# Attention probabilities transposed in twenty 64-row pieces instead of ten whole blocks

## The chip, the cores and the metric

The kernel runs on one core of one Trainium2 chip. Times are device microseconds of the whole program. The core's engines are TensorE (PE for its matmuls, PEld for its weight loads), VectorE (DVE), ScalarE (ACT), GpSimd (POOL) and SyncE (SP); they run side by side and meet at semaphores.

## The reference, cut to what matters

A block of a graph network on 625 nodes of 512 features, in two layers with a mixture of experts between them. Three stages of it are attention over all nodes with 8 heads of 64: one of the first layer's expert block, and two of the graph transformer, in which the sum over edges is taken as a masked attention over all 625 x 625 pairs of nodes.

```
q = (x @ Wq + bq).reshape(b, s, H, HD)
k = (x @ Wk + bk).reshape(b, s, H, HD)
v = (x @ Wv + bv).reshape(b, s, H, HD)
scores = jnp.einsum('bqhd,bkhd->bhqk', q, k) / jnp.sqrt(jnp.float32(HD))
attn = jax.nn.softmax(scores, axis=-1)
o = jnp.einsum('bhqk,bkhd->bqhd', attn, v).reshape(b, s, d) @ Wo + bo
...
hp = h @ weight
msgs = hp[src] * edge_weight[:, None]
agg = jax.ops.segment_sum(msgs, dst, num_segments=h.shape[0])
```

All of it is in fp32. The second excerpt is a sum over 20000 edges; the kernel builds a matrix of counts and weights out of the edge list, on which both the sum and the masks of the later attention rest.

## The kernel before

The 625 nodes are cut into NC = 5 chunks of NP = 125 rows. A stage of attention (`attention`, defined once for each engine, called with a = 0 for the expert block and with a = 1 and 2 for the graph transformer) handles the heads in PAIRS = 4 pairs and the nodes in 5 chunks, so it has 20 rounds u. For each round there are two score tiles `Sx[u % 3][h]` of 125 x 625, one for each head h. TensorE's order in round u is written out by hand:

- `scores(u + 2)`: q times k of both heads into PSUM banks 0 to 2 (L828). The heads lie on rows 0 to 63 and 64 to 127 of the array.
- `projection(i + 1, n)`: one or two pieces of the next pair's q, k and v (L805, L810). In the last pair of a stage (rounds u = 15 to 19) there is none.
- in the last two rounds `early`, a product of the stage behind (L624 in the first stage, L1033 in the others).
- `context(u - 1)`: the transposed probabilities times v (L859), two heads in the two column halves of the array, into bank 5.
- `turned(u)`: the probabilities transposed, five blocks of 125 x 125 for each head. Four of each head go to bank 3 + h (L841), the fifth ones to bank 5 (L848). A transpose is a matmul whose weights are the block and whose moving operand is the identity.

VectorE runs in round u `scaled(u + 1)` (L1630 to L1635, probabilities times the reciprocal sum), `largest(u + 2)` (L1622, scores with the mask out of PSUM, and their extreme), the values of the next pair, and `context_out(u - 1)` (L1642). ScalarE runs `turned_out(u - 1)` (L1241 twice and L1245: the transposed blocks out of PSUM into `PT`), then `exponentials(u + 2)` (L1233) and parts of the projections. The semaphores that matter here: `prob` (a head's probabilities are ready), `pT` (transposes written), `pTc` (copied out), `av` and `ctx` (context written, copied out). The first transposes into bank 3 + h wait for the copies out of the same bank, those into bank 5 for the copy out of bank 5 and for `ctx`.

The edge windows are another part. At the start VectorE works out, for each of NW = 20 windows of target nodes, the first and the last tile of edges; `window_ranges` (L350 to L356) loads these 2 x 20 values into registers on TensorE's and on VectorE's queue. TensorE does so behind the product `hp` (L624), VectorE behind the operations that make the one-hot rows (L1505). Then comes the loop over windows: VectorE makes a one-hot tile (L1516) and TensorE multiplies it (L682, L692).

After an attention stage the gates of the experts are a product with `gateW` and `gateW1` (L907), 32 columns of weights each and a padding of zeros.

## Time and profile before

| | |
|---|---|
| time, median of 3 runs | 1142.01 us (1137.84 to 1142.13) |
| the profiled execution, span from first to last instruction | 1134.8 us |
| TensorE busy | 1087.0 us, 96% |
| weight loads busy | 728.6 us, 64% |
| VectorE busy | 560.2 us, 49% |
| ScalarE busy | 371.2 us, 33% |
| GpSimd busy | 126.9 us, 11% |
| granted TensorE clock, mean | 1.000 |

The page of the profile gives busy times and a chain of work that ended last. The timeline gives groups of like instructions in order of time: start, time from the first one's start to the last one's end, engine, line, operation and count; in brackets the idle time before the group and what ended it. Ends of matmuls are modelled, so groups that follow each other seem to overlap by some 0.2 us: the starts are what one reads. PEldq and DVEq are the queues (sequencers) of TensorE and VectorE, which fetch values, check and branch.

### The profile page before, as it was taken

The numbers are of one execution on the slowest core, as the hardware profiler recorded it, in microseconds if no ns is written. First come the engines' busy times: TensorE is split into PE (matmuls) and PEld (weight loads), VectorE is DVE, ScalarE is ACT, GpSimd is POOL, SyncE is SP. The second block draws the span as 40 slices with busy tenths as digits, with TensorE's granted clock in tenths as the row PEclk, the third lists the DMA queues.
The fourth block names the chain that finished last, engine by engine and source line by source line (L and its number), as shares of the span: only waits on it lengthen the run. The fifth ranks groups of instructions, "written<-read, shape, count | busy, mean of one in ns | idle before, by whom it ended". The sixth has DMA issues, their size and how long they took to land.

```text
span 1134.8 us, 20059 instructions
## 1 busy us (share of the span) xinstructions
PE 1087.0 (96%) x7339; PEld 728.6 (64%) x7340; DVE 560.2 (49%) x1409; ACT 371.2 (33%) x931; POOL 126.9 (11%) x183
## 2 busy tenths in 40 slices
PE   3899999999999988999999899999999999999999
PEld 2588646468777554455545577887577778755764
DVE  7999738645445421121211444553324455587641
ACT  1012212035555412122212445453124455412630
POOL 1045460020000020010101530000000000001000
PEclk9999999999999999999999999999999999999999
DMA  4100475000000379800899840000210100000001
GB/s 133 38 1 3 131 201 213 1 28 29 19 11 1 155 248 409 332 14 18 330 400 403 295 167 29 29 29 1 75 56 29 29 29 1 1 37 1 1 3 43
DMA packets 21402, 112.69 MB, mean 99 GB/s; under 512 B 5127, under 2 KB 6904, under 8 KB 15198
## 3 DMA queue, kind: packets, MB, share of 16 engines
q1 hardware_dynamic: 15864, 100.95, 23.7%
q0 software_dynamic: 5472, 10.83, 3.6%
q8 instruction: 45, 0.74, 0.3%
q14 instruction: 21, 0.17, 0.1%
HBM read 102.78 MB, written 8.98 MB: 98 GB/s over the span
## 4 chain that ended last, share of the span: by engine, by line
PE 84%; DMA 5%; DVE 5%; issue 2%; ACT 2%; POOL 1%; DVEq 1%; SPq 0%; POOLq 0%
PE psum L624 11%; PE psum L805 10%; PE psum L1002 7%; PE psum L979 6%; PE psum L828 6%; PE psum L692 6%; PE psum L859 6%; PE psum L810 5%; PE psum L841 5%; PE psum L1129 3%; PE psum L1033 3%; DMA arena<-in_moeW 3%; PE psum L642 3%; PE psum L1107 3%; PE psum L762 2%
## 5 line engine op out<-in xcount | busy, mean ns | idle before, releaser
L624 PE MATMUL psum<-arena 128*125 128x512 f32 x320 | 140.0, 593 | 0.8 <-ACT arena L1203 0.7
L1233 ACT ACTIVATE arena<-arena,small 125x625 f32<-125x625 f32 x120 | 97.0, 809 | 89.9 <-DVE small L1622 89.9
L805 PE MATMUL psum<-arena 128*128 128x313 f32 (+1 forms) x384 | 110.0, 435 | 2.3 <-ACT arena L1171 1.4
L1308 ACT ACTIVATE arena<-psum,cols 128x64 f32<-128x64 f32 x224 | 47.4, 358 | 183.3 <-PE psum L988 183.3
L624 PEld LDWEIGHTS psum<-arena 128*125 128x125 f32 x320 | 59.2, 187 | 73.7 <-issue 69.6
L979 PE MATMUL psum<-arena 128*64 128x512 f32 x448 | 99.2, 594 | 6.1 <-DMA arena<-in_moeW 4.4
L1002 PE MATMUL psum<-arena 128*64 128x256 f32 x896 | 100.4, 381 | 3.0 <-DMA arena<-in_moeW 2.9
L805 PEld LDWEIGHTS psum<-arena 128*128 128x128 f32 x384 | 69.9, 189 | 31.2 <-ACT arena L1171 2.5
L1622 DVE CUSTOM_DVE_ANT_0 arena<-psum,cnt_adj 125x625 f32<-125x625 f32 x80 | 61.5, 806 | 55.0 <-PE psum L828 55.0
L1241 ACT ACTIVATE arena<-psum 125x500 f32<-125x500 f32 x120 | 63.8, 583 | 73.2 <-PE psum L841 73.2
L1002 PEld LDWEIGHTS psum<-arena 128*64 128x64 f32 x896 | 63.1, 137 | 36.3 <-issue 4.5
L828 PE MATMUL psum<-arena 64*125 64x113 f32 x480 | 80.3, 453 | 0.0
L859 PE MATMUL psum<-arena 125*64 125x125 f32 x1200 | 77.4, 274 | 0.5
L1516 DVE TENSOR_SCALAR arena<-arena 125x628 bf16<-125x628 f16 x222 | 76.1, 419 | 1.0 <-PE psum L682 0.6
L692 PE MATMUL psum<-arena 125*128 x1110 | 71.9, 220 | 4.1 <-DVE arena L1516 1.4
L859 PEld LDWEIGHTS psum<-arena 125*64 125x64 f32 x1200 | 63.2, 136 | 18.6 <-issue 13.1
L979 PEld LDWEIGHTS psum<-arena 128*64 128x64 f32 x448 | 31.7, 137 | 65.7 <-issue 58.3
L692 PEld LDWEIGHTS psum<-arena 125*128 125x128 bf16 x1110 | 62.2, 98 | 12.3 <-issue 10.7
L828 PEld LDWEIGHTS psum<-arena 64*125 64x125 f32 x480 | 52.5, 183 | 24.9 <-issue 16.1
L841 PE MATMUL psum<-ident,arena 125*125 125x125 f32 x480 | 67.9, 284 | 0.0
L841 PEld LDWEIGHTS psum<-ident,arena 125*125 125x125 f32 x480 | 57.1, 188 | 10.0 <-issue 9.5
L1642 DVE COPY arena<-psum 128x125 f32<-128x125 f32 x60 | 17.2, 286 | 91.7 <-PE psum L859 91.7
(299 smaller groups left out, 1422.2 us busy)
## 6 DMA issues: line engine op xcount, KB each, us to landing
arena<-in_moeW SPq DMA_DIRECT2D x32, 2048.0 KB, 18.2
arena<-in_att SPq DMA_DIRECT2D x36, 256.0 KB, 2.7
arena<-in_l1W SPq DMA_DIRECT2D x2, 2048.0 KB, 11.2
token_rows<-arena POOLq DMA_DIRECT2D x19, 128.0 KB, 4.9
rows<-in_rows SPq DMA_DIRECT2D x1, 2240.0 KB
expert_rows<-arena POOLq DMA_DIRECT2D x17, 128.0 KB, 4.8
arena<-in_gnnWo SPq DMA_DIRECT2D x2, 1024.0 KB, 5.6
arena<-token_rows POOLq DMA_DIRECT2D x14, 128.0 KB, 6.8
```

The costliest lines, as they stand in the source:

```text
L624: mm = pe.matmul(bank(b, NP, D), srcT[:, k, c * NP:(c + 1) * NP], w[:, k, :], start=(k == 0), stop=(k == KC - 1))
L692: mm = pe.matmul(psum[:, o + c * P:o + (c + 1) * P], one_src[:, s, c * NP:c * NP + P], hot_dst[:, bass.ds(e * P, P)], start=False, stop=False,
L805: mm = pe.matmul(bank(b, P, width), aw[:, w, k, :], srcT[:, k, o:o + width], start=(k == 0), stop=(k == KC - 1))
L828: mm = pe.matmul(psum[0:NP, at_:at_ + n], q[h * HD:(h + 1) * HD, c * NP:(c + 1) * NP], k[h * HD:(h + 1) * HD, o:o + n], start=True, stop=True)
L841: mm = pe.transpose(bank(3 + h, NP, NP, NP * j), Sx[u % 3][h][:, j * NP:(j + 1) * NP], ident[0:NP, 0:NP])
L859: mm = pe.matmul(psum[h * HD:(h + 1) * HD, 5 * 512 + 256:5 * 512 + 256 + NP], vv[i % 2][:, j, h * HD:(h + 1) * HD], PT[:, u % 2 * NC + j, ...
L979: mm = pe.matmul(psum[q * TT:(q + 1) * TT, 512 * b:512 * b + D], xsT[:, k4, :], EW1[par][:, k4, o:o + D], start=(k4 == 0), stop=(k4 == KC ...
L1002: mm = pe.matmul(psum[q * TT:(q + 1) * TT, 4 * 512:4 * 512 + D // 2], hT[:, f, :], EW2[par][:, f, q * (D // 2):(q + 1) * (D // 2)], start= ...
L1233: act.activation(Sx[u % 3][h], Sx[u % 3][h], ACT.Exp, bias=small[0:NP, 80 + n:81 + n], scale=-1.0, accum_out=small[0:NP, 120 + n:121 + n]) ...
L1241: act.activation(PT[:, u % 2 * NC:u % 2 * NC + 4, h * NP:(h + 1) * NP], bank(3 + h, NP, 4 * NP).rearrange("p (j n) -> p j n", j=4), ACT.Co ...
L1516: ve.tensor_scalar(one_src[:, s, :], iota_src[:, 0:SW], float(1024 * w), key[:, bass.ds(e, 1)], ALU.add, ALU.is_equal).then_inc(hot_ready, 1)
L1622: ve.tensor_tensor_reduce(Sx[u % 3][h], psum[0:NP, o:o + N], mask, 1.0, NO_EDGE / 10, ALU.add, ALU.min, small[0:NP, 80 + n:81 + n]).then_i ...
```

## The change

1. `turned(u)` transposes in twenty pieces instead of ten blocks. `QROWS` cuts the 125 rows of a block into rows 0 to 63 and 64 to 124; group g of rows lies in row group g of the array. A piece has 125 weight columns as before and 64 or 61 moving columns. Pieces of group 0 go to bank 3 and those of group 1 to bank 4, 64 columns each, with both heads in one bank; the fifth blocks go to bank 5 in 64-column slots as before with both groups. The order alternates between the groups. As no two groups may write bank 5 at once, a new semaphore `low` makes TensorE wait for its own last group-0 piece of bank 5 before the group-1 pieces of it that come last.
2. The wait for the copies out of banks 3 and 4 comes first, for both. The wait for bank 5 and `ctx` comes after eight pieces; before, it came after eight whole blocks.
3. `turned_out` copies by row group: bank 4 first, then bank 3, each with a four-dimensional pattern (512 and 488 elements a row for 500 and 500), then bank 5 (256 for 250). `PT` has slots of 128 columns instead of 125, the arena is 16 columns bigger, and `context` reads at the new offsets.
4. `window_ranges` loads the first 20 values with a lower bound of GT and with the runtime check of bounds, which it had skipped; the second 20 are loaded as before.
5. The two gate weights share one tile, so that one's padding is the other's weights and the padding at the end is shared.

```diff
+QROWS = [(0, 64), (64, NP)]
...
-        gateW = sb("gateW", [P, KC * EX + WMIN])
-        gateW1 = sb("gateW1", [P, KC * EX + WMIN])
+        gates = sb("gates", [P, 2 * KC * EX + WMIN])
+        gateW, gateW1 = gates[:, 0:KC * EX + WMIN], gates[:, KC * EX:]
...
-        PT = at(o_p, NP, 2 * NC, 2 * NP)
+        PT = at(o_p, NP, 2 * NC, 2 * P)
...
-            first, second = [nc.values_load_multi_w_load_instructions(
-                bounds[0:1, o:o + NW], engines=[engine], min_val=-NW * KG * GT, max_val=NW * KG * GT,
+            first = nc.values_load_multi_w_load_instructions(
+                bounds[0:1, 0:NW], engines=[engine], min_val=GT, max_val=NW * KG * GT)[1]
+            second = nc.values_load_multi_w_load_instructions(
+                bounds[0:1, NW:2 * NW], engines=[engine], min_val=-NW * KG * GT, max_val=NW * KG * GT,
                 skip_runtime_bounds_check_because="the program clamps a window's first tile and its count")[1]
-                for o in (0, NW)]
...
                 def turned(u):
 
-                    for h in range(2):
-                        pe.wait_ge(s["prob"], 2 * u + h + 1)
-                        if u:
-                            pe.wait_ge(s["pTc"], 3 * (u - 1) + h + 1)
-                        for j in range(4):
-                            mm = pe.transpose(bank(3 + h, NP, NP, NP * j), Sx[u % 3][h][:, j * NP:(j + 1) * NP],
-                                              ident[0:NP, 0:NP])
-                        mm.then_inc(s["pT"], 1)
+                    def piece(g, h, j):
+                        r0, r1 = QROWS[g]
+                        o = 512 * (3 + g) + 64 * (4 * h + j) if j < 4 else 512 * 5 + 64 * (2 * h + g)
+                        return pe.transpose(psum[0:NP, o:o + r1 - r0], Sx[u % 3][h][r0:r1, j * NP:(j + 1) * NP],
+                                            ident[r0:r1, r0:r1])
+
+                    pe.wait_ge(s["prob"], 2 * u + 1)
+                    if u:
+                        pe.wait_ge(s["pTc"], 3 * (u - 1) + 2)
+                    for j in range(4):
+                        piece(0, 0, j)
+                        piece(1, 0, j)
+                    pe.wait_ge(s["prob"], 2 * u + 2)
                     if u:
                         pe.wait_ge(s["pTc"], 3 * u)
                         pe.wait_ge(s["ctx"], u)
-                    for h in range(2):
-                        mm = pe.transpose(bank(5, NP, NP, NP * h), Sx[u % 3][h][:, 4 * NP:N], ident[0:NP, 0:NP])
-                    mm.then_inc(s["pT"], 1)
+                    piece(0, 0, 4)
+                    piece(1, 1, 0)
+                    piece(0, 1, 4).then_inc(s["low"], 1)
+                    piece(1, 1, 1)
+                    piece(0, 1, 0)
+                    piece(1, 1, 2)
+                    piece(0, 1, 1)
+                    piece(1, 1, 3).then_inc(s["pT"], 1)
+                    piece(0, 1, 2)
+                    pe.wait_ge(s["low"], u + 1)
+                    piece(1, 0, 4)
+                    piece(0, 1, 3).then_inc(s["pT"], 1)
+                    piece(1, 1, 4).then_inc(s["pT"], 1)
...
-                    for h in range(2):
-                        act.wait_ge(s["pT"], 3 * u + h + 1)
-                        act.activation(PT[:, u % 2 * NC:u % 2 * NC + 4, h * NP:(h + 1) * NP],
-                                       bank(3 + h, NP, 4 * NP).rearrange("p (j n) -> p j n", j=4),
+                    slot = u % 2 * NC
+                    for g in (1, 0):
+                        act.wait_ge(s["pT"], 3 * u + (1 if g else 3))
+                        n = QROWS[g][1] - QROWS[g][0]
+                        act.activation(PT[:, slot:slot + 4, :].rearrange("p j (h g n) -> p h j g n", h=2, g=2)[:, :, :, g, 0:n],
+                                       bank(3 + g, NP, 512).rearrange("p (h j n) -> p h j n", h=2, j=4)[:, :, :, 0:n],
                                        ACT.Copy).then_inc(s["pTc"], 1)
-                    act.wait_ge(s["pT"], 3 * u + 3)
-                    act.activation(PT[:, u % 2 * NC + 4, :], bank(5, NP, 2 * NP), ACT.Copy).then_inc(s["pTc"], 1)
+                    act.activation(PT[:, slot + 4, :], bank(5, NP, 2 * P), ACT.Copy).then_inc(s["pTc"], 1)
```

## Rows read from the trace of the kernel before

**Rows 1.** The page: busy time of each engine, and the chain that ended last.

```profile
PE 1087.0 (96%) x7339; PEld 728.6 (64%) x7340; DVE 560.2 (49%) x1409; ACT 371.2 (33%) x931; POOL 126.9 (11%) x183
...
PE 84%; DMA 5%; DVE 5%; issue 2%; ACT 2%; POOL 1%; DVEq 1%; SPq 0%; POOLq 0%
```

**Rows 2.** Timeline of TensorE, a middle round: start us, us, engine, line, operation.

```profile
294.77 1.14 PE L841 MATMUL psum<-ident,arena 125*125 125x125 f32 x8
295.75 0.38 PE L848 MATMUL psum<-ident,arena 125*125 125x125 f32 x2
296.06 1.34 PE L828 MATMUL psum<-arena 64*125 64x113 f32 x8
297.33 2.38 PE L805 MATMUL psum<-arena 128*128 128x313 f32 x8
```

**Rows 3.** Timeline, a transpose followed by a product in the undivided shape.

```profile
358.44 0.38 PE L848 MATMUL psum<-ident,arena 125*125 125x125 f32 x2
358.66 1.90 PE L624 MATMUL psum<-arena 128*125 128x512 f32 x4
```

**Rows 4.** Timeline of the weight loads, 296.05 to 296.10 and 296.10 to 296.20.

```profile
296.06 0.19 PEld L828 LDWEIGHTS psum<-arena 64*125 64x125 f32 x2
...
296.06 0.30 PEld L828 LDWEIGHTS psum<-arena 64*125 64x125 f32 x4
```

**Rows 5.** Line L963 alone: duration min, median, max ns, starts, forms.

```profile
L963 PE MATMUL psum<-ident,arena x56: 222/223/251, 415.3 to 627.6; 64*128 64x64 f32 x56
```

**Rows 6.** Timeline, the last ordinary round and the start of one without projection.

```profile
345.31 0.60 PE L859 MATMUL psum<-arena 125*64 125x125 f32 x8
345.84 1.14 PE L841 MATMUL psum<-ident,arena 125*125 125x125 f32 x8
345.95 0.29 DVE L1642 COPY arena<-psum 128x125 f32<-128x125 f32 x1 [0.81 <-PE psum L859]
...
347.12 1.34 PE L828 MATMUL psum<-arena 64*125 64x113 f32 x8
...
350.90 1.34 PE L828 MATMUL psum<-arena 64*125 64x113 f32 x8
```

**Rows 7.** Timeline, the rounds without projection that follow.

```profile
352.43 0.80 DVE L1622 CUSTOM_DVE_ANT_0 arena<-psum,ident 125x625 f32<-125x625 f32 x1
...
356.33 0.80 DVE L1622 CUSTOM_DVE_ANT_0 arena<-psum,ident 125x625 f32<-125x625 f32 x1
...
357.46 1.14 PE L841 MATMUL psum<-ident,arena 125*125 125x125 f32 x8
...
357.79 0.28 DVE L1642 COPY arena<-psum 128x125 f32<-128x125 f32 x1
```

**Rows 8.** Timeline, the last two rounds of the first stage.

```profile
363.43 1.14 PE L841 MATMUL psum<-ident,arena 125*125 125x125 f32 x8
...
363.87 0.26 DVE L1642 COPY arena<-psum 128x125 f32<-128x125 f32 x1
...
370.86 0.45 PE L848 MATMUL psum<-ident,arena 125*125 125x125 f32 x2 [0.36 <-ACT arena L1241]
```

**Rows 9.** Lines L968 and L352 on the queues, and the timeline from 20 to 46.

```profile
L968 PEldq FUSED_REGOPS  x12: 51/151/168, 403.9 to 617.5; - x12
L968 PEldq SEQ_ASSERT  x8: 18/18/18, 404.2 to 617.7; - x8
...
L352 DVEq TENSOR_LOAD <-arena x2: 4496/4616/4737, 25.9 to 30.6; - x2
L352 PEldq TENSOR_LOAD <-arena x2: 4747/4835/4923, 32.8 to 37.8; - x2
...
42.69 0.22 PE L682 MATMUL psum<-arena 125*128 125x64 f16 x2 [2.03 <-DVE arena L1505]
```

**Rows 10.** Groups by line and form, TensorE, 18.1 to 21.4 and 21.7 to 22.3.

```profile
L610 PE MATMUL psum<-ident,arena 125*128 125x125 f32 x15 | 3.4, 419 | 0.3 <-DVE arena L1439 0.3
...
L610 PE MATMUL psum<-ident,arena 125*128 125x125 f32 x5 | 0.8, 298 | 0.0
```

## What the change does to the time, predicted

> **What bounds the kernel.** I read the page first: of the span of 1134.8 us TensorE is busy in 96% of it, and 84% of the chain that ended last is TensorE's [rows 1]. So a nanosecond off TensorE's path is worth a nanosecond, and the other engines matter only where they make it wait. The diff touches two places, and I looked at each on the timeline. The first is attention, three stages of some 137 us, with 60 rounds in all (20 each). A round in the middle shows five blocks with no idle time between them: context (L859), ten transposes (L841 and L848), scores (L828), projection (L805 or L810), context [rows 2]. The reader is to see two starts: transposes begin at 294.77, scores at 296.06, the projection at 297.33. So the transposes cost 1.29 us and the scores 1.27 us, 2.55 us together after rounding. The second place is the start of the edge-window loop, where TensorE fetches 40 loop bounds from memory.
>
> **Where the 2.55 us of transposes and scores go.** From the first L848 transpose to the scores it is 0.31 us for two, while to the L624 product, which uses the array undivided as the transposes do, it is 0.22, so the pace is 0.11 [rows 2, 3]. The eight L841 transposes take 0.98 us, 0.10 more than eight at that pace: the first has a weight load that nothing covers, and its follower starts some 0.21 after it. So 0.09 us is the price of going over to scores of 64 rows, and the scores' first load is then uncovered as well, 0.10. The two heads' scores share the array: two weight loads of 64x125 lie within 0.19 us, the length of one, and four within 0.30 [rows 4]. So two row groups load side by side, every 0.106 us.
>
> **Attention, step by step.** (a) Twenty pieces in ten pairs. Each piece loads 125 weight columns, as the whole transposes did, and streams 64 columns instead of 125. A transpose that streams 64 columns is through in 0.223 us [rows 5], but a pair can't follow faster than its loads, 0.106. The second pair starts at 0.21, the tenth at 0.21 + 8 x 0.106 = 1.06, the scores at 1.16: 0.13 less than 1.29. (b) The scores find the array in their own shape and their first load done under the last pair. One 0.10 of it falls on the path: 1.17 for 1.27. With rounding, (a) and (b) give -0.22 us a round.
>
> The Trainium skill, "TensorE: Matmul & The Clock Gate", section LDWEIGHTS, says that a load takes the time of its columns, whatever its rows, and "TensorEngine Tiling (Array Packing)", section Performance Considerations, warns not to take the tiling factor from a dimension that is already small. By these rules halving the rows halves nothing in a load, and twice as many are needed; that is the first rival below. The loads in pairs in the trace speak against its happening.
>
> (c) **The wait on "low".** TensorE waits before pair nine for its own piece in pair six. That piece starts at 0.63, ends 0.22 later [rows 5], and a wait takes about 0.05 to be noticed (context ends at 345.91, the copy starts at 345.95) [rows 6]: 0.90. Pair nine's load was due with pair eight at 0.84. So 0.06 late in one row group; what is queued behind is pair nine's second half, pair ten and the scores. I take 0.05; bounds 0 and 0.15 (a whole uncovered load on top).
> (d) **The wait on the context copy**, which guards bank 5, moves from after eight whole transposes (0.98 us in) to after four pairs (load due at 0.42). The copy ends at 345.95 + 0.29 = 346.24, noticed at 346.29, that is 0.45 after the transposes' start at 345.84 [rows 6]. Cost 0.04; bounds 0 and 0.15.
> (e) The three copies out of PSUM by ScalarE read 512, 488 and 256 columns for 500, 500 and 250: nothing. But the first can start only after pair eight, some 0.4 us later than now. It is covered while a projection (1.7 us or more) stands between scores and the next context; if it were not, it would cost that 0.4.
>
> Sum for an ordinary round: -0.22 + 0.05 + 0.04 = -0.13 us. There are 45 (the first 15 of each stage): **-5.9 us**. The others give something back. The first round of a stage comes from a projection with no change of shape before it, and will now have one: +0.20, three times, 0.6. In rounds 16 and 17 no projection covers anything, and the chain of softmax on VectorE and ScalarE sets a period of 3.90 us (L1622 starts at 352.43 and 356.33) against TensorE's 3.78 (scores at 347.12 and 350.90) [rows 6, 7]: nothing gained, nothing lost. The last three rounds are followed by products in the undivided shape, so the change of shape is added instead of removed, +0.20 each. Round 18 meets the context copy behind L1622: 357.79 + 0.28 + 0.05 = 358.12 against a load due at 357.46 + 0.42 = 357.88, so +0.24 more [rows 7]; with (c) and the 0.03 that (a) keeps, +0.46, three times, 1.4. In the first stage rounds 19 and 20 find the copy behind a layer norm: 364.18 against 363.85 is +0.33, in all +0.55; in round 20 TensorE waits until 370.86 already, and six pairs (0.64) instead of two transposes (0.29) follow, with the change of shape again +0.55 [rows 8]. That is 1.1. The four such rounds of the other stages, where the copy is prompt, give +0.26 each, 1.0. Attention: -5.9 + 0.6 + 1.4 + 1.1 + 1.0 = **-1.8 us**.
>
> **The window bounds.** The first 20 values lose their skip of the runtime check. What a check costs shows at L968, where a value is loaded and checked: FUSED_REGOPS of 0.15 us at 403.9, then a SEQ_ASSERT of 0.02 at 404.2, with the gap between them and one like it behind about 0.29 in all; L352, the loads of the bounds, has none of either now [rows 9]. Twenty are 5.8 us on VectorE's and on TensorE's queue. VectorE hides them: its loads end at 30.6 + 4.5 = 35.1, and L1505, which was issued before them, holds L682 back until 42.5 anyway. TensorE doesn't: its second load ends at 37.8 + 4.7 = 42.5, just as late, and L682 starts at 42.69. The window loop on both engines, and all that follows, starts **5.8 us** later. Bounds: 0.3 (one fused check) and 7. Then TensorE is idle for about 8 us instead of 2.03. The first 15 transposes of the program, ahead of which TensorE had almost nothing to do for 18 us, took 0.419 us each and those after them 0.298 [rows 10], which fits the lower of the clock's two levels (1.2 and 2.4 GHz), though the granted clock is printed as 1.00 throughout. They lasted 3.2 us. Window matmuls at half pace would need 0.55 us a tile where VectorE delivers one in 0.29: about five tiles lost, **+1.5 us**; bounds 0 and 3.
>
> The rest (one tile for both gates, a bigger arena, memsets split) adds no instruction on the path: nothing.
>
> **Sum:** -1.8 + 5.8 + 1.5 = +5.5 us on a span of 1134.8. The median of the runs, 1142.0, lies 7.2 above the span, outside of what is changed, so the time is **1147.5 us**.
>
> **Rivals.**
> 1. *The pieces don't pair.* If transposes' loads in the two row groups follow one another, twenty of them take 20 x 0.106, 1.06 us more per round, 63 us over 60: 1210 us. For it: the rule above, and that the trace has only pairs that are no transposes. Against: loads of the same 64x125 form in pairs [rows 4]. It decides as soon as loads start 0.1 apart. Chance 0.07.
> 2. *The waits cost a restart each.* If either wait lets the queue run dry, the next load is uncovered: 0.10 each. For it: L848 took 0.45 after a wait where it takes 0.38 [rows 2, 8]. Over 45 rounds 9 us: 1156. It decides if the semaphore comes later than 0.1 us after the load was due. Chance 0.17.
> 3. *The checks cost nothing* (fused, or under the product before them) and the clock stays up: 1142.0 - 1.8 = 1140.2. For it: TensorE's queue runs ahead of the array by some 8 us there. Against: the loads already use all of that. Chance 0.16. If the two waits are free too, 4 us less, 1136. Chance 0.05.
>
> **Chances and range.** The forecast has 0.55, with a range of its own of 1143.5 to 1151. The range of 1139 to 1156 takes in rival 2 and the dearer part of rival 3, and leaves out rival 1 and the last one. About 0.5% (5.7 us) is what a measurement of this kernel can tell from no change: 1136.3 and 1147.7. Half of the forecast and rivals 1 and 2 lie above: slower 0.50. Half of the last rival and little more lie below: faster 0.04. The remainder, 0.46, is no difference.
>
> **What would show it.** In the profile after: the new transpose line with 1200 pieces in pairs, about 1.16 us from its first to the scores, and scores that take 1.17; if loads stand 0.1 apart, rival 1. Idle time of TensorE ahead of the transposes that is ended by L1642 or by the pieces themselves prices (c) and (d). At L352 (its new lines) 20 SEQ_ASSERTs on TensorE's queue, and L682's first start near 48.5 instead of 42.69; after it, matmuls at half pace for some 3 us. I would be wrong most cheaply in the checks: without them the sign turns.

## The result, and the profile after

The changed kernel takes **1145.84 us** in the median of nine runs (1143.24 to 1147.27), the kernel before, on the same chip, 1140.50 in nine (1137.76 to 1146.02). The ratio is 1.0053, with a 95% interval of 1.0038 to 1.0068, estimated from all these runs (the two medians alone give 1.0047): **slower by 5.3 us**. That is a small but clear loss, and it lies at the 0.5% (5.7 us) that the prediction took for the limit of what can be told from no change. The forecast was 1147.5 us, 5.5 more than before, and the range of 1139 to 1156 holds the result. The sum held; some of its terms in attention didn't, as the following shows.

The page of the changed kernel has the span, the busy time of TensorE and the chain that ended last, which answer to [rows 1]:

```profile
span 1143.5 us, 21282 instructions
...
PE 1087.9 (95%) x7939; PEld 732.4 (64%) x7940; DVE 561.1 (49%) x1409; ACT 372.7 (33%) x931; POOL 128.8 (11%) x183
...
PE 83%; DMA 7%; DVE 4%; issue 2%; ACT 2%; DVEq 1%; POOL 1%; SPq 0%; POOLq 0%; ACTq 0%
```

TensorE has 600 instructions more and 0.9 us more of busy time, in a span that is 8.7 us longer. So nearly all of the lost time is idle time of TensorE, and not work. 8.7 us is also more than the 5.3 between the medians. The profiled execution of before had a granted clock of 1.000 over its span, while the median of 25 other runs of it is 0.998, and it was some 3.5 us faster than their median. Where two traces are compared below, this is to be kept in mind.

**The start of the window loop.** First the two loads of bounds on TensorE's queue, each line alone (duration min, median, max in ns, then the first and last start), then TensorE's longest wait at that place (us in total, times, longest); before it was [rows 9].

```profile
L353 PEldq FUSED_REGOPS  x20: 146/146/165, 37.8 to 43.3; - x20
L353 PEldq SEQ_ASSERT  x20: 18/18/26, 38.0 to 43.5; - x20
...
L353 PEldq TENSOR_LOAD <-arena x1: 4923/4923/4923, 32.8 to 32.8; - x1
...
L355 PEldq TENSOR_LOAD <-arena x1: 4745/4745/4745, 43.5 to 43.5; - x1
...
L685 PEld LDWEIGHTS psum<-arena x40: 97/98/106, 48.4 to 125.3; 125*128 125x128 bf16 x40
```

```profile
PE psum L685 <- issue: 7.8, 1, 7.8
```

The twenty checks stand between 37.8 and 43.5, 0.28 us for each. The second load follows them, and the first window matmul starts at 48.4 where it started at 42.69 [rows 9]. "issue" says that nothing in the trace but TensorE's own queue held it back. Then the clock (columns: stretch, its length, busy time and instructions of PE, PEld, DVE, ACT, POOL, granted clock, DMA share, GB/s):

```profile
40.00:45.00 5.00, 0.68 (x2) 0.00 (x0) 2.81 (x1) 0.60 (x1) 0.00 (x0) 1.00 0.57 210
45.00:50.00 5.00, 0.82 (x8) 0.70 (x9) 1.11 (x4) 0.00 (x0) 0.00 (x0) 0.53 0.00 0
50.00:55.00 5.00, 5.00 (x50) 5.00 (x48) 4.00 (x12) 0.00 (x0) 0.00 (x0) 0.50 0.02 3
55.00:60.00 5.00, 5.00 (x86) 4.88 (x85) 4.61 (x15) 0.00 (x0) 0.00 (x0) 0.95 0.00 0
```

From about 45 until 55 us the granted clock is 0.5, which is 1.2 GHz of 2.4. TensorE handles 50 matmuls between 50 and 55 and 86 in the next stretch of the same length. The first window's last matmul comes 7.4 us later than before (64.50 against 57.07): 5.75 of it was there when the loop started, and the other 1.7 came within the window, which lasts 16.06 us for 14.38.

**A middle round of attention.** TensorE's timeline, as in [rows 2]:

```profile
301.94 1.43 PE L842 MATMUL psum<-ident,arena 64*125 64x64 f32 x20
303.17 1.33 PE L831 MATMUL psum<-arena 64*125 64x113 f32 x8
304.42 0.53 PE L808 MATMUL psum<-arena 128*128 128x313 f32 x1
```

Twenty pieces take 1.23 us to the scores, where the ten transposes took 1.29. The scores take 1.25 to the projection, where they took 1.27. With the third decimal of the starts the two blocks together took 2.553 us and take 2.484: **0.07 us a round** is gained, where 0.13 was forecast.

The starts of the weight loads show where the pieces lose time. These are three narrow stretches of the timeline of PEld, at the first, the fourth and the fifth pair:

```profile
301.94 0.18 PEld L842 LDWEIGHTS psum<-ident,arena 64*125 64x125 f32 x2 [0.17 <-issue]
...
302.26 0.19 PEld L842 LDWEIGHTS psum<-ident,arena 64*125 64x125 f32 x2
...
302.46 0.21 PEld L842 LDWEIGHTS psum<-ident,arena 64*125 64x125 f32 x2
```

Two loads stand together each time: the pieces pair. Three pairs go by in 0.32 us, 0.107 for each, and then it is 0.20 to the fifth. That is the wait on the context copy, and it costs 0.09 at the load and 0.07 at the matmul; e7 and e10 below confirm the cause, as the gap goes when the wait is gone or stands later.

**Rounds without a projection behind them.** In the fifteenth round of a stage the scores are followed by the context block at once. The timeline of the changed kernel, with the idle time before an instruction and what ended it in brackets:

```profile
352.44 1.43 PE L842 MATMUL psum<-ident,arena 64*125 64x64 f32 x20
...
353.66 1.33 PE L831 MATMUL psum<-arena 64*125 64x113 f32 x8
353.73 1.07 ACT L1261 ACTIVATE arena<-psum 125x488 f32<-125x488 f32 x2 [1.79 <-PE psum L842]
...
354.68 0.39 ACT L1264 ACTIVATE arena<-psum 125x256 f32<-125x256 f32 x1
...
355.12 1.05 PEld L877 LDWEIGHTS psum<-arena 125*64 125x64 f32 x20 [0.32 <-ACT arena L1264]
```

And the same round before, whose transposes start at 345.84 and whose scores start at 347.12 [rows 6]:

```profile
346.63 1.07 ACT L1241 ACTIVATE arena<-psum 125x500 f32<-125x500 f32 x2 [1.28 <-PE psum L841]
...
348.39 1.05 PEld L859 LDWEIGHTS psum<-arena 125*64 125x64 f32 x20
```

ScalarE's first copy starts 1.29 us after the first piece, before it was 0.79. The last copy ends at 355.07, and context's first load waits for it. From scores to context it is now 1.46 us, before it was 1.27.

### The profile page after: what moved, and what is told of

It is laid out like the page before. It is cut to its first block, busy times and chain, and to the rows that moved or that the text cites. A ratio compares the mean times of both kernels' runs of the same rounds, so it can differ in the third digit from the quotient of the medians.

```text
span 1143.5 us, 21282 instructions
## 1 busy us (share of the span) xinstructions
PE 1087.9 (95%) x7939; PEld 732.4 (64%) x7940; DVE 561.1 (49%) x1409; ACT 372.7 (33%) x931; POOL 128.8 (11%) x183
## 4 chain that ended last, share of the span: by engine, by line
PE 83%; DMA 7%; DVE 4%; issue 2%; ACT 2%; DVEq 1%; POOL 1%; SPq 0%; POOLq 0%; ACTq 0%
PE psum L627 11%; PE psum L808 9%; PE psum L1020 7%; PE psum L842 6%; PE psum L695 6%; DMA arena<-in_moeW 6%; PE psum L877 5%; PE psum L997 5%; PE psum L831 5%; PE psum L813 5%; PE psum L1051 3%; PE psum L1147 3%; PE psum L645 3%; PE psum L1125 3%; PE psum L765 2%
## 5 line engine op out<-in xcount | busy, mean ns | idle before, releaser
L1261 ACT ACTIVATE arena<-psum 125x488 f32<-125x488 f32 x120 | 64.0, 585 | 100.8 <-PE psum L842 100.2
L842 PE MATMUL psum<-ident,arena 64*125 64x64 f32 (+1 forms) x1200 | 86.1, 278 | 1.0 <-DVE arena L1661 1.0
L842 PEld LDWEIGHTS psum<-ident,arena 64*125 64x125 f32 (+1 forms) x1200 | 76.9, 184 | 12.9 <-issue 12.0
L695 PEld LDWEIGHTS psum<-arena 125*128 125x128 bf16 x1110 | 65.0, 100 | 11.3 <-issue 10.2
```

The costliest lines, as they stand in the source:

```text
L695: mm = pe.matmul(psum[:, o + c * P:o + (c + 1) * P], one_src[:, s, c * NP:c * NP + P], hot_dst[:, bass.ds(e * P, P)], start=False, stop=False,
L842: return pe.transpose(psum[0:NP, o:o + r1 - r0], Sx[u % 3][h][r0:r1, j * NP:(j + 1) * NP], ident[r0:r1, r0:r1])
L1261: act.activation(PT[:, slot:slot + 4, :].rearrange("p j (h g n) -> p h j g n", h=2, g=2)[:, :, :, g, 0:n], bank(3 + g, NP, 512).rearrange( ...
```

## The experiments

The ratios are to the kernel before, run on the same chip beside each. The runs were made on three chips: the median of before is 1140.19 beside e1 to e4, 1140.14 beside e5, e6, e7 and e9, and 1137.91 beside e8, e10 and e11. So where kernels from different chips are compared, the ratios are safer than the medians. By the trace the window start costs about 7 us and attention gains or loses less than 1, so the first runs separate the two places.

**e1: the checks alone.** The kernel before with the checked load of the change:

```diff
-            first, second = [nc.values_load_multi_w_load_instructions(
-                bounds[0:1, o:o + NW], engines=[engine], min_val=-NW * KG * GT, max_val=NW * KG * GT,
+            first = nc.values_load_multi_w_load_instructions(
+                bounds[0:1, 0:NW], engines=[engine], min_val=GT, max_val=NW * KG * GT)[1]
...
```

> The kernel before with one part of the change alone: the first 20 window bounds are loaded with the runtime check (transposes, copies and gates stay as they were). Theory: the checks stand on TensorE's path and cost 5.7 us, and the idle stretch that they make costs another 1.5 us at half clock, so about 7.3 us over the kernel before (ratio 1.0064), the window loop starting near 48.4 instead of 42.7, and the attention rounds as before (1.284 us for the transposes, 1.27 for the scores). Rival: the difference comes from the transposes, and the checks are hidden under the product before them; then this kernel takes the time of the kernel before (ratio 1.000, within 0.1%).

Measured: 1144.29 us (7 runs) against 1140.19 (25): 1.0032 (1.0021 to 1.0043), and a span of 1141.8. Its first window matmul, and the granted clock behind it:

```profile
L683 PE MATMUL psum<-arena x40: 193/193/237, 49.1 to 124.8; 125*128 125x64 f16 x40
...
45.00:50.00 5.00, 0.27 (x2) 0.14 (x2) 0.48 (x2) 0.00 (x0) 0.00 (x0) 0.65 0.08 31
50.00:55.00 5.00, 4.92 (x61) 4.93 (x62) 4.37 (x15) 0.00 (x0) 0.00 (x0) 0.67 0.01 3
```

The checks alone make the kernel slower, with the late start and the low clock. By the profiles they cost 7.0 us, by the medians 4.1, which is well under the 7.3 (1.0064) expected. The medians are what a user gets; the difference is mostly the fast profiled execution of before. The low clock also cost less here than in the changed kernel: from the start of the loop the first window takes 14.9 us, 0.5 more than before. The start itself is 0.6 later than the checks explain, because the product ahead of them ended at 41.3 and not at 40.7.

**e2 and e9: the checks, hidden.** e2 is the changed kernel with the checked values fetched in two lots of ten, behind the third and fourth chunk of the product "hp" and so under its matmuls; e9 does the same with the whole transposes of before.

```diff
-            product_rows("hp", T1, 0)
-            pe.wait_ge(range_ready, 1)
-            ends, shifts = window_ranges(mybir.EngineType.PE)
...
+            for c in range(NC):
+                product_chunk("hp", T1, ring[0], c)
+                if c == 2:
+                    pe.wait_ge(range_ready, 1)
+                if c in (2, 3):
+                    ends += first_tiles(mybir.EngineType.PE, (c - 2) * (NW // 2), NW // 2)
+            shifts = tile_shifts(mybir.EngineType.PE)
```

> The changed kernel with the same loads and the same checks, but TensorE's queue meets them earlier: ten values behind the third of the five chunks of the product hp, ten behind the fourth, the 20 shifts behind the fifth. Theory: the queue then fetches and checks while the array still has work; the window loop starts at 42.7 to 43.5, the granted clock stays 1.00, and the time falls by 6.5 to 7.3 us from the changed kernel, to 0 to 1 us over the kernel before (ratio 1.000 to 1.001). Rival: the checks are not what costs; then it takes the time of the changed kernel (ratio 1.005).

> The kernel before (whole transposes) with the checked bounds, and the loads moved up between the chunks of hp, the same loads as in the run of the changed kernel with earlier loads. It stands against that one in the transposes, copies and gates alone, and against the run with the checks alone in the place of the loads alone. Theory: the loads now cost nothing, so it takes the time of the kernel before or 1 us less (ratio 0.999 to 1.000), and the changed kernel with earlier loads (0.9994) is within 1 us of it: the pieces bring nothing. Rival: the pieces cost 2 us by themselves, as the medians of the changed kernel (1.0053) and of the checks alone (1.0032) suggest; then this kernel comes out near 0.9975.

Measured: e2 1138.67 us (12 runs), 0.9994 (0.9982 to 1.0005); e9 1138.37 (12 runs), 0.9998 (0.9978 to 1.0018). e2's first window matmul:

```profile
L695 PE MATMUL psum<-arena x40: 189/193/193, 42.9 to 118.6; 125*128 125x64 f16 x40
...
45.00:50.00 5.00, 5.00 (x65) 5.00 (x62) 4.27 (x14) 0.00 (x0) 0.00 (x0) 0.66 0.01 3
```

The loop starts at 42.9 again, and e2 is some 7 us faster than the changed kernel. By the medians all of the loss was in the late start. A stretch at a lower clock remains, against the expectation (0.66 between 45 and 50), and the window's end is still 0.7 us late. e2 and e9 differ by the transposes, copies and gates alone, and are the same within their intervals: **the pieces bring nothing that can be measured**.

That they cost nothing isn't shown. Four of e9's twelve executions had a granted clock of 0.986 to 0.990 and took 1140.3 to 1145.7 us; all of e2's had 0.997 or more. The other eight of e9 have a median of 1137.1, which is 0.9973 of before and so near the rival's 0.9975. At like clocks the pieces may cost 1 to 2 us. Picking executions afterwards isn't a test, so this stays open.

**e8: the clock by itself.** The changed kernel with three fp32 matmuls, whose result nobody reads, between TensorE's checks and its second load.

```diff
-            ends, shifts = window_ranges(mybir.EngineType.PE)
+
+            def keep_busy():
+                for _ in range(3):
+                    pe.matmul(bank(3, P, D), onesf[0:NP, :], N1[:, 0, :], start=True, stop=True)
+
+            ends, shifts = window_ranges(mybir.EngineType.PE, keep_busy)
```

> The changed kernel with three matmuls of 125x512 into bank 3, whose result nobody reads, between TensorE's checked loads of bounds and its second load; they take some 1.3 us of array each and end well before the first window matmul, so they delay nothing. It tells what the lower granted clock behind the checks costs by itself. If the 7.8 us without a matmul are what brings the clock down, the granted clock stays at 1.00 (or clearly above the 0.50 to 0.53 of the changed kernel) between 45 and 60 us, the first window matmul still starts near 48.4, and the end of the first window comes 1.0 to 1.7 us earlier than in the changed kernel. If the clock comes from elsewhere, it is 0.50 there again and nothing moves.

Measured, in one run: 1145.01 us, span 1143.1. The same stretches as above:

```profile
40.00:45.00 5.00, 2.15 (x5) 0.79 (x4) 2.51 (x1) 0.60 (x1) 0.00 (x0) 0.86 0.54 192
45.00:50.00 5.00, 3.70 (x12) 1.46 (x11) 0.78 (x3) 0.00 (x0) 0.00 (x0) 0.80 0.04 18
50.00:55.00 5.00, 4.83 (x82) 4.35 (x79) 5.00 (x18) 0.00 (x0) 0.00 (x0) 1.00 0.01 3
```

Now 82 matmuls run between 50 and 55 where there were 50. The values of 0.86 and 0.80 are means over 5 us: the clock was at 0.5 from 43.6 to 47.0 us, at the start of the fillers and ahead of the window loop, and full when the loop began. The fillers took 4.4 us for the three, where I had expected 1.3 each. The loop started 0.4 us later (48.82), yet the first window ended 1.6 us earlier, at 62.89. So the lower clock costs 1.6 to 2.0 us in the profiled execution of the changed kernel, against 1.5 forecast.

Other executions paid less for it. The checks stand in the same place in e1, e3, e6, e7 and e10, and their profiles have a low clock of 7 to 10 us there too, but their first window lasts only 14.8 to 15.0 us, 0.4 to 0.7 more than the 14.38 of before. Nor is the long idle time the whole cause. e2 and e9, whose loop starts on time, have a drop between 45 and 50 as well and lose 0.5 us by it, while e4, with the same loads, has none:

```profile
45.00:50.00 5.00, 4.80 (x80) 4.24 (x78) 4.97 (x18) 0.00 (x0) 0.00 (x0) 1.00 0.02 3
```

What these profiles show is that the drop is longer behind the 7.8 us without a matmul (7 to 10 us at 0.5, in six kernels) than without them or with fillers (0 to 3.4 us, in seven).

The whole span of e8 is only 0.4 us shorter, so most of the gain was given back later: it is 1.5 us ahead in the first stage of attention and 0.4 at the start of the second. What lies between is the experts' stage with its waits for DMA, and one run doesn't tell more.

**e6: no neighbours in different row groups.** The changed kernel with ten pieces of the upper rows, then ten of the lower.

```diff
                     for j in range(4):
                         piece(0, 0, j)
-                        piece(1, 0, j)
...
+                    for j in range(4):
+                        piece(0, 1, j)
+                    for j in range(4):
+                        piece(1, 0, j)
```

> The changed kernel with the same twenty pieces in another order: all ten of row group 0, then all ten of row group 1. Theory: only neighbours in different row groups load side by side, so the pieces follow each other every 0.105 to 0.109 us and the turn of a round takes 2.1 to 2.2 us instead of 1.165 (rival 1 of the prediction, made on purpose), about 50 us in all. If the queue finds its pairs by itself further ahead, the turn stays at 1.2 us.

Measured, in one run: 1190.1 us, span 1188.2. A middle round on TensorE:

```profile
305.32 1.77 PE L842 MATMUL psum<-ident,arena 64*125 64x64 f32 x17
306.82 0.36 PE L831 MATMUL psum<-arena 64*125 64x113 f32 x1
...
308.46 0.80 PE L808 MATMUL psum<-arena 128*128 128x313 f32 x2
```

From the first piece to the projection it is 3.14 us in place of 2.48; the last pieces of the lower rows lie among the scores of the upper ones. 0.66 us in 60 rounds is 40 us, of the 44 by which the run is slower than the changed kernel. The expectation had 2.1 to 2.2 us for the turn and 50 us in all. The last piece starts only 1.83 us after the first: by the single records the first lower piece starts at 0.80, with three upper ones still to start. So pieces of the two groups overlap over a few places, and not only as neighbours, but far from all of them do. That is rival 1 brought about: what the pieces gain rests on their order in the program.

**e7: the two waits gone.** The changed kernel with the pieces of the fifth blocks written to banks 3 and 4. These overwrite other blocks, and the copy of bank 5 reads bank 3, so the fifth blocks' probabilities are left out of context; "low" and the early wait on the context copy fall away. ScalarE's copies also wait for the last piece now, which costs where no projection covers them, so the middle rounds are what is compared and not the whole time.

```diff
-                        o = 512 * (3 + g) + 64 * (4 * h + j) if j < 4 else 512 * 5 + 64 * (2 * h + g)
+                        o = 512 * (3 + g) + 64 * (4 * h + j % 4)
...
-                    pe.wait_ge(s["low"], u + 1)
```

> The changed kernel with the causes of its two new waits taken away: the pieces of the fifth blocks go to banks 3 and 4 over others instead of to bank 5, so neither the wait for the context copy nor the one for the own piece is needed (what is copied for the fifth blocks is then wrong data, so only the rounds of the first attention stage are read). Theory: the pairs come every 0.109 us throughout; from the first pair to the last 0.158 + 8 x 0.109 = 1.03 us instead of 1.165, and the scores behind take 1.21 instead of 1.256 since the second head's row group is not late any more; 0.18 us a round. Rival: the waits are covered and the round stays as it is.

Measured, in one run: 1141.05 us, span 1139.1.

```profile
300.05 1.30 PE L842 MATMUL psum<-ident,arena 64*125 64x64 f32 x20
301.19 1.29 PE L831 MATMUL psum<-arena 64*125 64x113 f32 x8
302.41 2.38 PE L808 MATMUL psum<-arena 128*128 128x313 f32 x8
```

1.14 us to the scores and 1.22 to the projection: 2.36 in place of 2.48. The waits cost 0.12 us a round, against 0.09 in the forecast and 0.18 expected of this run. The last pair starts 1.03 us after the first, as expected, and the scores follow it by one more pace of 0.109.

**e3 and e5: loads of 128 columns.** If the loads set the pace, a shorter load quickens it. In the trace of before the transposes of L963 [rows 5] load 128 columns in 139 ns. An ordinary product's load of 128 columns, at L805, takes 189:

```profile
L963 PEld LDWEIGHTS psum<-ident,arena x56: 137/139/222, 415.2 to 627.5; 64*128 64x128 f32 x56
...
L805 PEld LDWEIGHTS psum<-arena x384: 186/189/190, 232.9 to 947.7; 128*128 128x128 f32 x192
```

e3 is the changed kernel with three more weight columns in 18 of the 20 pieces (they fill three more PSUM partitions that nobody reads). e5 is e9 with the same in nine of the ten whole transposes.

```diff
-                        return pe.transpose(psum[0:NP, o:o + r1 - r0], Sx[u % 3][h][r0:r1, j * NP:(j + 1) * NP],
-                                            ident[r0:r1, r0:r1])
...
+                        c0 = o_s + (2 * (u % 3) + h) * N + j * NP
+                        return pe.transpose(psum[:, o:o + r1 - r0], arena[r0:r1, c0:c0 + P], ident[r0:r1, r0:r1])
```

> The changed kernel with one size changed: all pieces but those of the last block of head 1 load 128 weight columns instead of 125 (three columns of the next block, which land in PSUM rows that nobody reads). Theory: what spaces the pairs is the weight load, and a transpose's load of 128 columns takes 0.139 us in the trace where one of 125 takes 0.183 to 0.189; so the pairs go from 0.109 to about 0.06, until the waits for the context copy and for the own piece bind (turn of a round 0.95 to 1.0 us instead of 1.165), 0.2 us in 45 rounds, 9 us in all (ratio to before 0.997). Rival: the pairs are spaced by the rate at which the queue can issue two loads and two matmuls; then the pace stays at 0.109 and nothing changes (ratio 1.005).

> The whole transposes with earlier loads, and 128 weight columns instead of 125 in nine of the ten. Theory: a whole transpose streams 125 columns in 0.104 us, so the faster load (0.139 against 0.189 us) saves only the uncovered half of the first load (0.05) and some 0.004 a transpose: 0.05 to 0.09 us a round, 3 to 5 us in 60 rounds less than the same kernel with 125 columns. Rival: the load sets nothing at all for whole transposes: no difference.

Measured: e3 1141.14 us (12 runs), 1.0006 (0.9996 to 1.0016), span 1138.3; e5 1134.71 (12 runs), 0.9960 (0.9946 to 0.9974), span 1132.1. The loads of e3's wide pieces, line alone:

```profile
L846 PEld LDWEIGHTS psum<-ident,arena x1080: 133/138/193, 263.2 to 986.2; 64*128 64x128 f32 x120, 61*128 61x128 f32 x60
```

and those of the changed kernel, also line alone:

```profile
L842 PEld LDWEIGHTS psum<-ident,arena x1200: 180/184/187, 263.7 to 991.5; 64*125 64x125 f32 x86, 61*125 61x125 f32 x86
```

A transpose's load of 128 columns takes 138 ns and one of 125 columns 184; in e5 the whole transposes' loads of 128 take 141. By the row of L805 an ordinary product wouldn't gain by padding. A middle round of e3, and then one of e5:

```profile
300.67 0.82 PE L846 MATMUL psum<-ident,arena 64*128 64x64 f32 x10
...
301.75 1.39 PE L831 MATMUL psum<-arena 64*125 64x113 f32 x8
303.06 1.85 PE L808 MATMUL psum<-arena 128*128 128x313 f32 x6
```

```profile
289.10 1.07 PE L852 MATMUL psum<-ident,arena 125*128 125x125 f32 x8
...
290.32 1.34 PE L839 MATMUL psum<-arena 64*125 64x113 f32 x8
291.58 0.53 PE L816 MATMUL psum<-arena 128*128 128x313 f32 x1
```

e3's pieces follow each other every 0.06 us while nothing holds them up, so the rate at which the queue issues would allow twice the pace. But then the context copy is late: pair five starts 0.55 us after the first, as in the changed kernel. The round takes 2.39, 0.09 less than in the changed kernel, which is 5.4 us in 60 rounds and 5.4 us by the ratios too, somewhat over half of what was expected. In e5 the whole transposes take 1.22 in place of 1.28 and wait for nothing; 0.06 in 60 rounds is 3.8 us, and e5 is 3.7 faster than e9 by the medians of the same chip.

The Trainium skill, "TensorE: Matmul & The Clock Gate", section LDWEIGHTS, has a load take the time of its columns. Its other half, that the rows don't count, agrees with the changed kernel's row: loads of 64 and of 61 rows all take 180 to 187 ns. Between 125 and 128 columns of a transpose this row and e3's say the opposite of the first half, and the measurement decides.

**e4: both.** e3 with the earlier loads of e2, and nothing else.

> Both edits of the two experiments before together: bounds loaded earlier and 128 weight columns. If they are independent, the gains add: 6.5 to 7.3 us plus what the wide pieces give by themselves (9 us by the theory of loads, 0 by the theory of issue), ratio to before 0.990 to 0.992 or 1.000 to 1.001.

Measured: **1133.39 us** (6 runs), 0.9936 (0.9918 to 0.9954), span 1133.0. That is the fastest kernel of the study, and faster than the kernel before and the changed one. The gains of e2 and e3 (0.0059 and 0.0047 off the ratio of 1.0053) add up to 0.9947, which lies within its interval; the 0.990 to 0.992 of the expectation doesn't. Its lead over e5, with whole transposes, is 1.3 us by the medians and 2.7 by the ratios, and the two intervals overlap.

**e10 and e11: the copy's wait moved back.** The changed kernel (e10) and e4 (e11) with the upper rows' pieces for bank 5 in pairs seven and eight. The lower rows' fifth pieces are the last two of all.

```diff
+                    for j in range(2):
+                        piece(0, 1, j)
+                        piece(1, 1, j)
                     if u:
                         pe.wait_ge(s["pTc"], 3 * u)
                         pe.wait_ge(s["ctx"], u)
                     piece(0, 0, 4)
...
                     piece(0, 1, 2)
+                    piece(0, 1, 3)
                     pe.wait_ge(s["low"], u + 1)
                     piece(1, 0, 4)
-                    piece(0, 1, 3).then_inc(s["pT"], 1)
-                    piece(1, 1, 4).then_inc(s["pT"], 1)
+                    piece(1, 1, 4).then_inc(s["pT"], 2)
```

> The changed kernel with another order of the last twelve pieces: the pieces that write bank 5 in row group 0 come in pairs seven and eight instead of five and six, so the context copy has two more pairs of time, and the wait on low has one pair less before it (one pair between the piece waited for and the piece that waits). Expected by prices of the changed kernel: the gap of 0.07 us at pair five goes; the low wait grows from 0.05 to some 0.15 to 0.20 in row group 1. Turn to scores 1.23 to 1.30 us (1.226 in the changed kernel), scores to next block 1.26 as before: ratio to the changed kernel 0.999 to 1.003. If instead the low wait is as cheap as it was, the turn takes 1.15 us and the kernel is 4 us faster than the changed one.

> The fastest kernel so far (bounds loaded earlier, pieces with 128 weight columns, 1133.4 us, 0.9936 of the kernel before) with the order of the run beside it. With pieces every 0.06 us the context copy came 0.25 us or more late at pair five; two more pairs ahead of it take up 0.12 us of that. The low wait stands then behind it with one pair between, 0.15 to 0.2. If the waits add up one after the other, the turn stays at 1.08 to 1.15 us and the time at 1133 to 1137; if the copy's wait was the one that counted, the turn falls to 0.98 to 1.02 us, 4 to 6 us less in all: 1128 to 1130.

Measured: e10 1154.56 us (5 runs), 1.0135 (1.0115 to 1.0155), span 1156.2; e11 1133.99 (6 runs), 0.9961 (0.9946 to 0.9976), span 1131.8. A middle round of e10:

```profile
303.94 1.46 PE L842 MATMUL psum<-ident,arena 64*125 64x64 f32 x19
305.09 0.36 PE L831 MATMUL psum<-arena 64*125 64x113 f32 x1
305.24 0.27 PE L842 MATMUL psum<-ident,arena 61*125 61x61 f32 x1
...
306.56 0.53 PE L808 MATMUL psum<-arena 128*128 128x313 f32 x1
```

The expectation for e10 was wrong. The gap of the copy's wait went as expected, but the round takes 2.61 us in place of 2.48. I had counted pairs and overlooked that the tail is now two upper pieces followed by two lower ones. Neighbours in the same row group don't load side by side, and the last piece starts 1.30 us after the first, behind a score. 0.13 us in the 45 rounds of this kind are 6 us, of 8.7 between the medians and 9.4 by the ratios. A further part is the clock, which was 0.986 to 0.992 in all five executions against 0.994 to 0.996 in the changed kernel. In the one profiled it was low in the experts' stage (this stretch of e10, and then the same of the changed kernel):

```profile
400.00:420.00 20.00, 19.37 (x76) 15.00 (x77) 5.75 (x27) 5.74 (x12) 4.81 (x4) 0.57 0.76 298
```

```profile
400.00:420.00 20.00, 17.66 (x106) 11.16 (x108) 8.26 (x34) 2.79 (x4) 6.00 (x5) 1.00 0.74 274
```

Why it fell there isn't settled; that four executions of e9, with the whole transposes, have as low a clock speaks against the pieces' order as the only cause. In e11 the round takes 2.39 as in e4, by the first of the two answers written for it: what the copy's wait gives back is lost in the tail. By the ratios e11 (0.9961) isn't as fast as e4 (0.9936), though the medians on their two chips lie 0.6 us apart.

## Why the prediction was right, and where it wasn't

**The checks (+5.8): right.** 0.28 us for each, 5.75 in all, the first window matmul at 48.4 for 48.5. e1 and e2 show it from both sides, by putting the checks in and by hiding them (4.1 us more by the medians, 7.2 less).

**The clock (+1.5): right for the profiled execution, too high for others.** The mechanism came: the clock at 0.5 and half as many matmuls. It cost 1.7 by the trace, 1.6 to 2.0 by e8, but 0.4 to 0.7 in the profiles of e1, e3, e6, e7 and e10, and 0.5 in e2 and e9, which don't have the long idle time. Together the start of attention is 7.5 us late (263.72 against 256.14, of which 0.09 belongs to the change of shape), where the sum had 7.3. What the sum left out is that the other runs of before are at a clock of 0.998 and aren't as fast as the one profiled.

**Attention (-1.8): wrong in sign.** By the difference of the starts in the two traces it is +0.8, and by e2 against e9 nothing. By its terms, each read from the starts in the two traces:

- *First fourteen rounds of each stage*, with the shape change in the first: forecast 42 x -0.13 + 0.6 = -4.9, measured -2.7. The size that failed most is (b): the scores were to gain 0.10 and gained 0.01. Without the waits they take 1.22 (e7), so half of the gain was never there, and the waits took 0.04 of the rest: head 1's row group, late by the wait on "low", starts its scores 0.05 behind head 0's. Why half of the first load stays uncovered isn't shown. My reading is that the last pieces' stream is shorter than a load, and no run varies it. (a) came out a little better: the second pair starts at 0.16 and not at 0.21, the pace is 0.109 for 0.106, and with no waits the turn takes 1.14 (e7) for 1.16. (c) and (d) were 0.05 and 0.04; the traces show 0.05 and 0.07, and e7 0.12 for the two. In (d) the copy ends 0.40 after the first piece, as computed, but the load behind it follows 0.12 later and not 0.05.
- *The fifteenth round*: forecast -0.13 three times, measured +0.13 three times. This is the step that failed as a mechanism. "(e) ... covered while a projection stands between scores and the next context" was right; but I counted the fifteenth round among the covered ones, and it is the first that has no projection. ScalarE's first copy starts 0.5 us later there, for some 0.4 in (e), and its last copy ends 1.41 us after the scores' start, for 0.85 before. The scores' own 1.27 us still cover most of that, so it costs context 0.20 and not the 0.4 that (e) named.
- *Rounds 16 and 17*: forecast nothing, measured 0.02 in all. The turn is 0.04 shorter and context waits that much longer.
- *Round 18*: forecast +1.4, measured +0.9; the copy of context was less late than computed, as it starts 0.15 us after the first piece, where before it was 0.33. *The last two of the first stage*: forecast 1.1, measured 1.2. Here the wait is on the context copy, as the timeline has it, in answer to [rows 8]:

```profile
370.44 0.65 PE L842 MATMUL psum<-ident,arena 64*125 64x64 f32 x8
371.28 0.43 PE L842 MATMUL psum<-ident,arena 64*125 64x64 f32 x4 [0.20 <-DVE arena L1661]
```

- *The four such rounds of the other stages*: forecast 1.0, measured 1.1.

The measured terms are -2.7 + 0.4 + 0.0 + 0.9 + 1.2 + 1.1 = +0.9, which is the +0.8 of the traces but for rounding.

**The rivals.** Rival 1 was rightly small: the loads pair as the scores' loads did, and e6 comes near its price, 44 us where I had worked out 63. Rival 2 didn't come: no wait cost a load's whole 0.10 over the forecast, but the two together came within 0.03 of what I gave them. Rival 3 fell with the twenty checks at L353.

**The sum and the median.** By the traces the change costs 8.7 us (7.5 + 0.8, and 0.4 between the stages), by the medians 5.3. That the forecast of 5.5 lies so near the latter is in good part luck, as two misses of some 3 us cancel. The sum was 3.2 too low against the traces (2.6 in attention, 0.2 at the start, 0.4 between the stages), and the profiled execution of before was 3.5 us too fast to stand for the median. I had put the 7.2 us between span and median down to work outside of the span. In every later run that is 1.9 us; of the rest 3.5 was the execution, and 1.8 that the median of the three runs at hand (1142.01) lies above that of 25 (1140.19).

It isn't settled why the checks alone cost 4.1 us by the medians of e1 and the whole change 5.3, which would give the pieces 1.2 us, while e2 and e9 differ by 0.3 (or by 1.5, at like clocks): all of this lies inside the intervals. Where the other executions of before lose their 3.5 us isn't known, as only one was profiled. That the runtime check can be skipped again in the changed kernel wasn't tried.

## What to carry to other kernels

Pieces in two row groups halve the rows of a load and double the count, so they pay only for what loads in pairs, and only while the program alternates between the groups, or nearly so (e6); a wait in the queue of such pieces held back both groups (the context copy's, 0.07 us) or the one with the load behind it ("low", 0.05). When a consumer's copy is moved behind more producers, go through the rounds one by one and name for each what covers it: the first round without cover is where the gain goes. And a runtime check on a loop bound is cheap only where matmuls are queued to hide it: twenty cost 5.75 us in the open and nothing measurable under a product (e2, e9).

## What the hardware showed that was not expected

- Loads of 128 columns of a transpose took 138 ns and those of 125 columns 184 (e3, e5). Three useless columns save 3.7 us in 60 rounds. Loads of 128 columns of an ordinary fp32 product take 189 (L805).
- Pieces in two row groups start every 0.06 us a pair when the loads allow it (e3), and every 0.109 with 125 columns.
- Instructions of one row group start ahead of earlier ones of the other: in e10 a score starts at 305.09, and the last piece, which stands before it in the program, at 305.24. In e6 the first lower piece starts while three upper ones ahead of it haven't.
- Behind 7.8 us without a matmul the granted clock was 0.5 for 7 to 10 us. In the changed kernel that cost 1.7 us, in five others 0.4 to 0.7. With three fp32 matmuls in the gap it was 0.5 for 3.4 us, and full before the window loop began (e8, one run).
